# Gated cross-attention and mixture-of-experts block, one core: the value product cut into three key chunks in three consecutive slots, and the next batch's preparation laid out anew over the slots

## The chip, the cores and the metric

The kernel runs on 1 core of one Trainium2 chip. The metric is the device time of one execution in microseconds (us), lower is better. The engines are TensorE (PE; its weight loads are shown apart, as PEld), VectorE (DVE), ScalarE (ACT), GpSimd (POOL) and SyncE (SP, which only issues DMAs here).

## The reference

Cut to what matters. B = 16 batches, S = 112 queries, S2 = 375 keys, D = 256 columns, 16 heads of 16 columns.

```python
q = split_heads(layernorm(x) @ wq + bq); k = split_heads(ctx @ wk + bk); v = split_heads(ctx @ wv + bv)
logits = einsum('bhqd,bhkd->bhqk', q, k) / 4 + (1 - mask) * -1e9
attn = softmax(logits) * group_prob            # group_prob is per batch, query and key
out = einsum('bhqk,bhkd->bhqd', attn, v)       # the value product
x = x + tanh(g_xattn) * (out @ wo + bo)
x = x + tanh(g_ffn) * ffn(layernorm(x))        # a shared FFN and the two best of 8 experts
```

## The kernel before

The kernel has a prologue (queries, weights and batch 0's keys and values), the attention over 16 batches, and then the output projection, routing and the expert FFN. Only the attention and the lines ahead of it are touched.

**Steps and slots.** The attention has one `step` for each batch t on every engine, two steps to a loop iteration, and 16 slots n in a step, one for each head. The order of work on an engine is written out by hand, so an engine that waits holds up everything behind it. In slot n of TensorE's step stand: the three transposes of head n's probabilities (`turn_probs`, L925; float32, 112 rows by 125 keys, one for each third of the keys) into bank `PT[n % 2]`; between them the scores of head n + 4 (`scores`, L912) into bank `SC[n % 2]`; and one slot of the preparation of the next batch, in three thirds (`prep_third`). The transposes of head n wait until the bank has been read for head n - 2.

**The other engines.** In slot n VectorE masks the scores of head n + 3 and takes their row maximum (`mask_scores`, L1227), and multiplies the turned probabilities of head n by the turned group probabilities into `probsT` (`weigh`, L1234). ScalarE takes the exponentials (L713). For the four heads of `POOL_HEADS` GpSimd multiplies by the group probabilities before the transposes instead (`times_group_prob`, L508), TensorE's transposes wait for that, and ScalarE only copies the turned result (`copy_probs`, L704) two heads later in its own order.

**The value product.** `values` (L943) takes four heads (a quad) at once: 3 key chunks by 4 heads = 12 float32 matmuls, each on its own 32 columns of the array (125 x 32 weights, 112 columns streamed); the trace shows two instructions for each, so 24. It stands in slots 1, 5, 9 and 13, after the slot's preparation; in slot 1 it is the last quad of the batch before. In slot 5 the row sums are turned behind it (`turn_sums`, L900).

**The preparation of a batch** runs through two PSUM banks, `PR[0]` and `PR[1]`, in seven pieces: the context turned (`turn_ctx`, L842, two pieces of 6 float16 transposes), the keys (`keys`, L854, two pieces of 6 matmuls over 375 columns), the values (`vals`, L878, with a bias matmul L876 ahead of each of the three chunks of 6 matmuls; chunks 0 and 1 are one piece in `PR[1]`, chunk 2 a piece in `PR[0]`) and the group probabilities turned (`turn_gp`, L863, 3 transposes). ScalarE takes every piece out of PSUM (`prep_piece`: L639, L644, L651, L654, L647), and for the keys VectorE takes the low part as well (`keys_low`, L1180). The slot of a piece is that of `prep_slot` less `PREP` = 4: keys in slots 15 (of the step before), 0, 1 and 2; nothing in 3, 4 and 14; values in 5 to 10; group probabilities in 11; context of the batch after the next in 12 and 13. The keys' high and low parts go through DRAM (`store_keys`, L299) and come back stacked (`stack_keys`, L308) before the batch's scores.

Of the kernel before, what the change touches and what calls it, by code (L numbers as in the profile page):

```python
# [35 lines left out]
PREP = 4  # L36
# [25 lines left out]
def flamingo_block(nc, x, ctx, gp, mask, g_xattn, g_ffn, wq, bq, wk, bk, wv, bv, wo, bo, nw, router,  # L62
# [9 lines left out]
    with ExitStack() as st:  # L72
# [116 lines left out]
        prep_mm, prep_act, prep_lo = sem("prep_mm"), sem("prep_act"), sem("prep_lo")  # L189
# [35 lines left out]
        POOL_HEADS = (2, 6, 8, 12)  # L225
# [9 lines left out]
        def turned_ctx(k):  # L235

            return ps[:, PR[k], 0:KC * P].bitcast(F16).rearrange("p (a c n) -> p a c n", a=2, c=KC)
# [7 lines left out]
        def _(sp):  # L245
# [46 lines left out]
            def store_keys(b, m):  # L292
                high, low = sp.compute_val(7 * b + 3 + m), sp.compute_val(2 * b + 1 + m)
# [69 lines left out]
            def step(t, p, more=True):  # L363
# [255 lines left out]
        def _(act):  # L619
# [16 lines left out]
            def prep_piece(b, k, p):  # L636
                act.wait_ge(prep_mm, 7 * b + k + 1)
                if k < 2:
                    act.activation(ctxT[:, :, k, 0:S2].rearrange("p a (c n) -> p a c n", c=KC), turned_ctx(k)[:, :, :, 0:KP],  # L639
                                   ACT.Copy).then_inc(prep_act, 1)  # L640
                elif k < 4:
                    if not (isinstance(b, int) and b == 0):
                        act.wait_ge(k_out[k - 2], 48 * b)
                    act.activation(kT[:, HI, k - 2], bank(PR[k - 2], P, S2), ACT.Identity,  # L644
                                   bias=bcol[:, k:k + 1]).then_inc(prep_act, 1)
                elif k == 6:
                    act.activation(gpT[:, p], bank(PR[1], KP, KC * S).rearrange("p (c q) -> p c q", c=KC), ACT.Copy).then_inc(prep_act, 1)  # L647
                elif k == 4:
                    if isinstance(b, int) and b == 0:
                        act.wait_ge(pad_zero, 2)  # L650
                    act.activation(head_columns(p, 0, 2), bank(PR[1], KP, 2 * D).rearrange("p (c h d) -> p c h d", c=2, h=H),  # L651
                                   ACT.Copy).then_inc(prep_act, 1)
                else:
                    act.activation(head_columns(p, 2, 3), bank(PR[0], KP, D).rearrange("p (c h d) -> p c h d", c=1, h=H),  # L654
                                   ACT.Copy).then_inc(prep_act, 1)
# [37 lines left out]
            prep_piece(0, 6, 0)  # L693
# [13 lines left out]
            pieces = {0: 1, 3: 2, 5: 3, 11: 4, 13: 5, 14: 6}  # L707

            def step(t, p, first=False, t_next=True, t_after=True):
                act.wait_ge(rr_made, t + 1)  # L710
                for n in range(H):
# [12 lines left out]
            prep_piece(1, 0, 1)  # L724
            step(0, 0, first=True)
            with act.Fori(0, B // 2 - 2) as i:
                step(2 * i + 1, 1)
                step(2 * i + 2, 0)
            step(B - 3, 1)
            step(B - 2, 0, t_after=False)  # L730
            step(B - 1, 1, t_next=False, t_after=False)
# [70 lines left out]
        def _(pe):  # L802
# [28 lines left out]
            def turn_ctx(b, k, third):  # L831
                if third == 0:
                    if k == 0:
# [3 lines left out]
                        else:  # L837
                            pe.wait_ge(prep_act, 7 * b - 1)
                    elif not (isinstance(b, int) and b == 0):
                        pe.wait_ge(prep_act, 7 * b)  # L840
                for a in range(2):
                    mm = pe.transpose(turned_ctx(k)[:, a, third, 0:KP], ctx_pair[:, a, third, k * P:(k + 1) * P], ident16[0:KP, 0:KP])  # L842
# [3 lines left out]
            def keys(b, m, part, third):  # L846

                if third == 0:
                    if m == 0:
                        pe.wait_ge(prep_act, 7 * b + 1 + part)  # L850
# [3 lines left out]
                mm = pe.matmul(bank(PR[m], P, S2), wpair[:, 1, w, part, m * P:(m + 1) * P], ctxT[:, a, part, 0:S2],  # L854
# [4 lines left out]
            def turn_gp(b, p, n, third):  # L859
                if third == 0:  # L860
                    pe.wait_ge(in_gp[p], 16 * n)
                    pe.wait_ge(prep_act, 7 * b + 5)
                mm = pe.transpose(ps[0:KP, PR[1], third * S:(third + 1) * S], gp_in[:, p, third * KP:(third + 1) * KP], ident[0:S, 0:S])  # L863
# [3 lines left out]
            def vals(b, c, part, third):  # L867

                if c == 0 and part == 0 and third == 0:
                    pe.wait_ge(prep_lo, 2 * b + 2)  # L870
                    if isinstance(b, int) and b == 0:
                        pe.wait_ge(w_lo, 5)
                        pe.wait_ge(ctx_pad, 1)
                to = ps[:, PR[0] if c == 2 else PR[1], c % 2 * D:c % 2 * D + D]
# [54 lines left out]
            def values(t, g, p):  # L929

                if g == 0:
                    pe.wait_ge(o_read, t + 1)
                    pe.wait_ge(prep_act, 7 * t + 7)
                four = range(g * QUAD, (g + 1) * QUAD)
                pe.wait_ge(pt_read, NDVE * t + by_dve(four[-1]) + PT_FREE)
                pe.wait_ge(pt_copied, NPOOL * t + by_pool(four[-1]))
                for c in range(KC):
                    for k in four:

                        h = ORDER[k]  # L940
                        half, row = h // (H // ND), h % (H // ND) // 2 * PAD
                        first = h * PAD + (DH if h % 2 == 0 else 0)
                        mm = pe.matmul(ps[row:row + PAD, OB[p], half * S:(half + 1) * S], values_pad[p][:, c, first:first + PAD],  # L943
                                       probsT[:, k % AT, c], start=(h % 2 == 0 and c == 0), stop=(h % 2 == 1 and c == KC - 1))
                mm.then_inc(av_made, 1)
# [4 lines left out]
            for n in range(2):  # L950
                prep_whole(0, n, 0, 1)
            queries(0)
            for n in range(2, 7):
                prep_whole(0, n, 0, 1)
            turn_x(Q_TILES[1])
            for n in range(7, H - 1):
# [5 lines left out]
            prep_whole(0, H - 1, 0, 1)  # L962
# [9 lines left out]
            for n in range(2):  # L972
# [4 lines left out]
            def step(t, p, loads, loaded, loaded_next, first=False, t_next=True, t_after=True):  # L977

                def prep_third(n, third):
                    if n + PREP < H and t_next:  # L980
                        prep_slot(t + 1, n + PREP, 1 - p, loads, third)
                    if n + PREP >= H and t_after:
                        prep_slot(t + 2, n + PREP - H, p, None, third)
# [33 lines left out]
            values(B - 1, H // QUAD - 1, 1)  # L1017
# [103 lines left out]
        def _(dve):  # L1121
# [56 lines left out]
            def keys_low(b, m):  # L1178
                dve.wait_ge(prep_act, 7 * b + 3 + m)
# [291 lines left out]
```

## Time and profile before

| | before |
|---|---|
| median of 3 runs | 702.06 us (701.38 to 702.97) |
| the profiled execution's own time | 701.34 us |
| its span, first to last instruction | 699.5 us |
| mean granted TensorE clock | 0.952 |
| attention, first to last transpose of probabilities | 48.5 to 343.2 us |
| one step in the steady part | 18.8 us |

The times are those of the whole launch; the span is some 1.8 us less than the execution's own time. A row of a timeline gives the start in us from the span's start, the duration, the engine, the line, the operation, what it writes and reads, its shape, and (if there was any) the idle time of the engine before it with what ended it. Matmuls are pipelined: a duration of 0.26 us is a latency, and what a matmul costs TensorE is the distance from its start to the next one's.

### The profile page before, as it was taken

Reading aid. Unit: us, or ns where it says so; the run is one execution under the profiler, and the core shown is the slowest. Engines: PE = TensorE matmul, PEld = TensorE weight load, DVE = VectorE, ACT = ScalarE, POOL = GpSimd, SP = SyncE. Lnnn points to the kernel's source line nnn. Section 1 sums busy time; section 2 is a strip of 40 time slices with the busy share of each in tenths; the row PEclk is TensorE's granted clock in tenths of the full one; section 3 lists DMA queues with packets and bytes.
Section 4 is the critical chain, followed back from the end, with each engine's and each line's share of the span. In section 5 each row is a group of like instructions: output and inputs, shape, how many; then the busy total and the mean of one; then the engine's idle time right before and its main releaser. Section 6 shows DMA issues by size and latency. Waiting matters only on the chain. (4 is left out here: it accounts for less than half of the span.)

```text
span 699.5 us, 19174 instructions
## 1 busy us (share of the span) xinstructions
PE 598.9 (86%) x6150; PEld 499.4 (71%) x6150; DVE 482.4 (69%) x1298; ACT 392.8 (56%) x994; POOL 281.7 (40%) x327
## 2 busy tenths in 40 slices
PE   2689999999999999999757999898999999799960
PEld 2457777777777778777536887787788788587850
DVE  6858777877777877778695766547555556556537
ACT  4368888888888888887716423144352444424320
POOL 7303444443443334446530178605345525355120
PEclk9799999999999999999975999999999999999995
DMA  8536557775555555632040042203434332341218
GB/s 219 153 81 144 151 138 188 184 197 135 132 130 137 138 141 138 155 87 68 1 181 1 9 152 84 98 23 116 141 110 147 107 120 91 120 138 46 61 49 311
DMA packets 86601, 84.29 MB, mean 121 GB/s; under 512 B 17879, under 2 KB 80341, under 8 KB 86430
## 3 DMA queue, kind: packets, MB, share of 16 engines
q1 hardware_dynamic: 78686, 70.83, 36.8%
q0 software_dynamic: 2976, 8.16, 3.2%
q10 hardware_dynamic: 4896, 4.76, 2.5%
q8 instruction: 23, 0.38, 0.2%
q14 instruction: 20, 0.16, 0.1%
HBM read 55.43 MB, written 28.30 MB: 120 GB/s over the span
## 5 line engine op out<-in xcount | busy, mean ns | idle before, releaser
L925 PE MATMUL ps<-ident,probs 112*125 112x112 f32 x768 | 192.6, 277 | 2.5 <-POOL probs L508 1.4
L713 ACT ACTIVATE probs<-probs,negmax 112x375 f32<-112x375 f32 x256 | 154.9, 608 | 26.0 <-DVE negmax L1227 25.8
L1079 PE MATMUL ps<-w,arena 128*128 128x256 f16 x1152 | 139.0, 277 | 20.8 <-DVE arena L1370 20.6
L763 ACT ACTIVATE arena<-ps,b 128x256 f32<-128x256 f32 x192 | 78.5, 473 | 138.8 <-PE ps L1068 138.8
L925 PEld LDWEIGHTS ps<-ident,probs 112*125 112x125 f32 x768 | 138.9, 188 | 23.6 <-issue 7.4
L1227 DVE CUSTOM_DVE_ANT_0 probs<-ps,neg 112x375 f32<-112x375 f32 x256 | 137.3, 538 | 11.8 <-issue 9.5
L1079 PEld LDWEIGHTS ps<-w,arena 128*128 128x128 f16 x1152 | 109.9, 99 | 45.6 <-DVE arena L1370 32.2
L508 POOL TENSOR_TENSOR probs<-probs,gp_in 112x375 f32<-112x375 f32 x64 | 58.6, 915 | 181.2 <-ACT probs L713 181.1
L1234 DVE TENSOR_TENSOR arena<-ps,gpT 125x336 f32<-125x336 f32 x192 | 97.0, 506 | 46.3 <-PE ps L925 45.7
L1068 PE MATMUL ps<-probs,w 128*128 128x256 f16 x816 | 91.9, 273 | 0.0
L1068 PEld LDWEIGHTS ps<-probs,w 128*128 128x128 f16 x816 | 79.9, 98 | 9.2
L912 PE MATMUL ps<-kst,arena 112*128 112x375 f16 x256 | 82.7, 324 | 2.3 <-DVEq L1214 1.3
L1370 DVE TENSOR_TENSOR arena<-arena 128x512 f16<-128x512 f32 x96 | 73.9, 770 | 3.3
L611 POOL DMA_INDIRECT y_back<-y_sb,dest x34 | 36.5, 1073 | 72.9 <-DVE y_sb L1434 66.6
L1368 DVE CAST arena<-arena 128x512 f16<-128x512 f32 x96 | 46.0, 479 | 25.0 <-ACT arena L763 24.8
L878 PE MATMUL ps<-wpair,ctxT 128*128 128x256 f16 x288 | 62.5, 281 | 0.0
L592 POOL DMA_INDIRECT x_sent<-qT,slots x28 | 32.8, 1172 | 52.5 <-issue 52.5
L943 PE MATMUL ps<-arena,w 125*32 125x112 f32 x1536 | 50.1, 263 | 0.7 <-DVE arena L1234 0.7
L713 ACT ACTIVATION_READ_ACCUMULATOR probs<-probs,negmax 112x1 f32 x256 | 50.0, 195 | 0.0
L854 PE MATMUL ps<-ctxT,wpair 128*128 128x375 f16 x192 | 49.4, 330 | 0.0
L581 POOL CAST w<-w2s 128x512 f16<-128x512 f32 x32 | 20.8, 649 | 67.8 <-DVE arena L1370 61.4
L943 PEld LDWEIGHTS ps<-arena,w 125*32 125x32 f32 x1536 | 34.6, 109 | 13.7 <-issue 11.2
(173 smaller groups left out, 829.8 us busy)
## 6 DMA issues: line engine op xcount, KB each, us to landing
k_scratch<-kT SPq DMA_DIRECT2D x96, 93.8 KB
kst<-k_scratch SPq DMA_DIRECT2D x64, 140.6 KB, 3.5
w1s<-in_L_ffn_ew_dram SPq DMA_DIRECT2D x8, 1024.0 KB, 4.9
w2s<-in_L_ffn_ew_dram SPq DMA_DIRECT2D x8, 1024.0 KB, 5.6
x_sent<-y_sb SPq DMA_DIRECT2D x12, 516.0 KB, 5.1
ctx_in<-in_ctx_dram SPq DMA_DIRECT2D x16, 375.0 KB
probs<-x_sent ACTq DMA_DIRECT2D x18, 258.0 KB, 2.6
arena<-y_back SPq DMA_DIRECT2D x7, 512.0 KB, 7.1
```

The source lines that it names most:

```text
L508: pool.tensor_tensor(probs[:, n % PROBS], probs[:, n % PROBS], gp_in[:, p], ALU.mult).then_inc(gp_times, 1)
L713: act.activation(probs[:, n % PROBS], probs[:, n % PROBS], ACT.Exp, bias=negmax[:, p, n:n + 1], scale=-1.0, accum_out=rowsum[:, p, ORDER[n ...
L763: act.activation(hid32[:, f], ps[:, f // 2 % 4, f % 2 * TILE:(f % 2 + 1) * TILE], ACT.Relu, bias=b1[:, f, e:e + 1]).then_inc(h_relu, 1)
L878: mm = pe.matmul(to, ctxT[:, a, part, c * KP:c * KP + P], wpair[:, 2, w, part], start=False, stop=(part == 1 and third == 2))
L912: pe.matmul(bank(SC[n % 2], P, S2), qb[0:PAIR, p, h // 2, h % 2], kst[0:PAIR, p, h // 2], start=True, stop=True).then_inc(sc_made, 1)
L925: mm = pe.transpose(ps[0:KP, PT[n % 2], c * S:(c + 1) * S], probs[:, n % PROBS, c * KP:(c + 1) * KP], ident[0:S, 0:S])
L943: mm = pe.matmul(ps[row:row + PAD, OB[p], half * S:(half + 1) * S], values_pad[p][:, c, first:first + PAD], probsT[:, k % AT, c], start=(h ...
L1068: mm = pe.matmul(ps[:, f // 2 % 4, f % 2 * TILE:(f % 2 + 1) * TILE], w1[:, p, w, k, f * P:(f + 1) * P], rows(a, k), start=(j == 0), stop=( ...
L1079: mm = pe.matmul(ps[:, 4 + a, 0:D], hid[:, u, f, a * P:(a + 1) * P], w2[:, p, w, f], start=(f == 0 and j == 0), stop=(f == NF - 1 and j == 2))
L1227: dve.tensor_tensor_reduce(probs[:, n % PROBS], bank(SC[n % 2], S, S2), neg[:, p], -1.0, BIG, ALU.add, ALU.min, negmax[:, p, n:n + 1]).the ...
L1234: dve.tensor_tensor(probsT[:, n % AT], bank(PT[n % 2], KP, KC * S).rearrange("p (c q) -> p c q", c=KC), gpT[:, p], ALU.mult).then_inc(pt_r ...
L1370: dve.tensor_tensor(hid[:, LO, two], hid32[:, two], hid[:, HI, two], ALU.subtract).then_inc(h_split, 1)
```

## The change

The value product is cut: `values` takes one key chunk c (4 matmuls, one for each head of the quad), and the three chunks stand in slots 1, 2 and 3, in 5, 6 and 7, and so on. The preparation is laid out anew: keys in slots 0 to 3, values in 5 to 10 with chunk 2 first, the group probabilities in 11, the context of the batch after the next in 13 and 14, and nothing in 4, 12 and 15. Its seven pieces now take the two banks strictly in turn, over the border between batches too (`prep_bank`). The group probabilities are copied out of PSUM by VectorE in its slot 11 (`take_group_probs`), no longer by ScalarE. ScalarE's pieces, VectorE's low keys and division, and `POOL_HEADS` (1, 5, 9, 13) move to other slots. SyncE stores a piece of the keys in two parts (high ones first) and stacks the first half before it stores the second. The prologue has the same pieces in the new order.

```diff
-        POOL_HEADS = (2, 6, 8, 12)
+        POOL_HEADS = (1, 5, 9, 13)
+        def prep_bank(p, piece):
+            return PR[(p + piece) % 2]
...
 def store_keys(b, m):
-                sp.wait_ge(prep_lo, low)
                 for n, c in enumerate(K_PARTS):
+                    if c == LO:
+                        sp.wait_ge(in_x[0], 16)
+                        sp.wait_ge(prep_lo, low)
                     sp.dma_start(heads[:, n * DH:(n + 1) * DH], kT[:, c, m]).then_inc(k_out[m], 16)
...
-                for m in range(ND):
-                    store_keys(t + 1, m)
+                store_keys(t + 1, 0)
                 if more:
                     next_mask(t + 1, 1 - p)
-                for m in range(ND):
-                    stack_keys(t + 1, 1 - p, m)
+                stack_keys(t + 1, 1 - p, 0)
+                store_keys(t + 1, 1)
+                stack_keys(t + 1, 1 - p, 1)
...
-            pieces = {0: 1, 3: 2, 5: 3, 11: 4, 13: 5, 14: 6}
+            pieces = {0: 0, 1: 1, 3: 2, 5: 3, 8: 4, 12: 5}
...
-                    if t_after and n == H - 1:
-                        prep_piece(t + 2, 0, p)
-                    if n == 8 and not first:
+                    if n == 9 and not first:
                         take_sums(t - 1, 1 - p)
...
 def turn_ctx(b, k, p, third):
                         else:
-                            pe.wait_ge(prep_act, 7 * b - 1)
+                            pe.wait_ge(prep_act, 6 * b)
                     elif not (isinstance(b, int) and b == 0):
-                        pe.wait_ge(prep_act, 7 * b)
+                        pe.wait_ge(gp_turned, b)
...
+            V_ORDER = (2, 0, 1)
+            def vals(b, c, part, p, third):
+                if part == 0 and third == 0:
+                    if c == 2:
+                        pe.wait_ge(prep_lo, 2 * b + 1)
+                    if c == 0:
+                        pe.wait_ge(prep_lo, 2 * b + 2)
...
+            CTX_SLOTS, V_SLOT, GP_SLOT = (13, 14), 5, 11
             def prep_slot(b, n, p, loads, third):
-                if n < 2:
-                    turn_ctx(b, n, third)
-                elif 3 <= n < 7:
-                    keys(b, (n - 3) // 2, (n - 3) % 2, third)
-                elif 9 <= n < 15:
-                    vals(b, (n - 9) // 2, (n - 9) % 2, third)
-                elif n == 15:
+                if n in CTX_SLOTS:
+                    turn_ctx(b, CTX_SLOTS.index(n), p, third)
+                elif n < 2 * ND:
+                    keys(b, n // 2, n % 2, p, third)
+                elif V_SLOT <= n < GP_SLOT:
+                    vals(b, V_ORDER[(n - V_SLOT) // 2], (n - V_SLOT) % 2, p, third)
+                elif n == GP_SLOT:
                     turn_gp(b, p, loads, third)
...
-            def values(t, g, p):
-                if g == 0:
-                    pe.wait_ge(o_read, t + 1)
-                    pe.wait_ge(prep_act, 7 * t + 7)
+            def values(t, g, p, c):
                 four = range(g * QUAD, (g + 1) * QUAD)
-                pe.wait_ge(pt_read, NDVE * t + by_dve(four[-1]) + PT_FREE)
-                pe.wait_ge(pt_copied, NPOOL * t + by_pool(four[-1]))
-                for c in range(KC):
-                    for k in four:
-                        ...
-                mm.then_inc(av_made, 1)
+                if c == 0:
+                    if g == 0:
+                        pe.wait_ge(o_read, t + 1)
+                        pe.wait_ge(prep_act, 6 * t + 6)
+                    pe.wait_ge(pt_read, NDVE * t + by_dve(four[-1]) + PT_FREE)
+                    pe.wait_ge(pt_copied, NPOOL * t + by_pool(four[-1]))
+                for k in four:
+                    ...
+                if c == KC - 1:
+                    mm.then_inc(av_made, 1)
...
-                    if first and n == 0:
-                        for m in range(2, PREP):
-                            prep_whole(t + 1, m, 1 - p, loads)
...
-                    if n % QUAD == 1:
+                    if n % QUAD >= 1:
                         if n > QUAD:
-                            values(t, n // QUAD - 1, p)
+                            values(t, n // QUAD - 1, p, n % QUAD - 1)
                         elif not first:
-                            values(t - 1, H // QUAD - 1, 1 - p)
+                            values(t - 1, H // QUAD - 1, 1 - p, n % QUAD - 1)
...
-            values(B - 1, H // QUAD - 1, 1)
+            for c in range(KC):
+                values(B - 1, H // QUAD - 1, 1, c)
...
+            def take_group_probs(b, p):
+                dve.wait_ge(prep_mm, 7 * b + 7)
+                dve.tensor_copy(gpT[:, p], bank(prep_bank(p, 6), KP, KC * S).rearrange("p (c q) -> p c q", c=KC)).then_inc(gp_turned, 1)
...
-                    if prep and n in (1, 3):
-                        keys_low(t + 1, n // 3)
+                    if prep and n in (2, 5):
+                        keys_low(t + 1, n // 5, 1 - p)
+                    if prep and n == 11:
+                        take_group_probs(t + 1, 1 - p)
-                    if n == 8 and not first:
+                    if n == 9 and not first:
                         divide(t - 1, 1 - p)
```

## Rows read from the trace of the kernel before

**Rows 1.** The page's part 1: busy time of each engine.

```profile
PE 598.9 (86%) x6150; PEld 499.4 (71%) x6150; DVE 482.4 (69%) x1298; ACT 392.8 (56%) x994; POOL 281.7 (40%) x327
```

**Rows 2.** Windows, one for each step: busy us (x instructions) by engine, clock, DMA.

```profile
68.13:86.95 18.82, 17.65 (x212) 14.79 (x211) 14.79 (x49) 15.34 (x45) 7.79 (x10) 1.00 0.56 152
...
274.89:293.65 18.76, 17.60 (x213) 14.75 (x211) 14.79 (x49) 15.34 (x45) 7.78 (x10) 1.00 0.64 158
293.65:312.08 18.43, 17.34 (x212) 14.76 (x211) 14.70 (x49) 15.39 (x45) 7.80 (x10) 1.00 0.35 84
312.08:329.30 17.22, 16.43 (x197) 13.54 (x196) 14.62 (x49) 13.95 (x43) 10.36 (x12) 1.00 0.28 69
329.30:343.00 13.70, 12.09 (x156) 9.40 (x156) 11.87 (x41) 10.74 (x33) 8.58 (x10) 1.00 0.01 2
```

**Rows 3.** Waits from 100 to 300 us: us in total, times, longest.

```profile
PEld ps L842 <- ACT gpT L647: 8.4, 11, 0.8
PEld ps L876 <- DVE kT L1180: 8.1, 11, 0.8
```

**Rows 4.** TensorE's timeline, slot 1 of one step and the start of slot 2.

```profile
219.41 0.26 PE L925 MATMUL ps<-ident,probs 112*125 112x112 f32 x1
219.51 0.32 PE L854 MATMUL ps<-ctxT,wpair 128*128 128x375 f16 x1
219.68 0.26 PE L925 MATMUL ps<-ident,probs 112*125 112x112 f32 x1
219.77 0.32 PE L912 MATMUL ps<-kst,arena 112*128 112x375 f16 x1
219.93 0.26 PE L925 MATMUL ps<-ident,probs 112*125 112x112 f32 x1
220.03 0.48 PE L854 MATMUL ps<-ctxT,wpair 128*128 128x375 f16 x2
220.44 0.78 PE L943 MATMUL ps<-arena,w 125*32 125x112 f32 x24
221.15 0.36 PE L925 MATMUL ps<-ident,probs 112*125 112x112 f32 x1
221.35 0.32 PE L854 MATMUL ps<-ctxT,wpair 128*128 128x375 f16 x1
```

**Rows 5.** TensorE's timeline of the step before: slots 5 to 8, parts.

```profile
207.33 0.41 PE L900 MATMUL ps<-ident,rrow 112*128 112x112 f32 x2
207.58 0.27 PE L925 MATMUL ps<-ident,probs 112*125 112x112 f32 x1
...
208.37 0.26 PE L925 MATMUL ps<-ident,probs 112*125 112x112 f32 x1
...
209.27 0.26 PE L925 MATMUL ps<-ident,probs 112*125 112x112 f32 x1
...
210.05 0.26 PE L925 MATMUL ps<-ident,probs 112*125 112x112 f32 x1
```

**Rows 6.** TensorE's timeline of the same step: slots 10, 12 and 13, parts.

```profile
212.41 0.38 PE L878 MATMUL ps<-wpair,ctxT 128*128 128x256 f16 x2
...
213.56 0.36 PE L925 MATMUL ps<-ident,probs 112*125 112x112 f32 x1
...
214.29 0.39 PE L842 MATMUL ps<-ident,ctx_pair 125*128 125x125 f16 x4
214.52 0.31 PE L925 MATMUL ps<-ident,probs 112*125 112x112 f32 x1
```

**Rows 7.** ScalarE's timeline of the same step.

```profile
211.12 0.60 ACT L651 ACTIVATE w<-ps 125x512 f32<-125x512 f32 x1
211.59 0.62 ACT L713 ACTIVATE probs<-probs,negmax 112x375 f32<-112x375 f32 x1
...
212.83 0.38 ACT L654 ACTIVATE w<-ps 125x256 f32<-125x256 f32 x1
```

**Rows 8.** GpSimd's timeline of the same step: head 12.

```profile
212.45 0.99 POOL L508 TENSOR_TENSOR probs<-probs,gp_in 112x375 f32<-112x375 f32 x1 [2.12 <-ACT probs L713]
```

More of the change, by code:

```diff
@@ L704, in copy_probs, with step @@
                 act.activation(probsT[:, n % AT], bank(PT[n % 2], KP, KC * S).rearrange("p (c q) -> p c q", c=KC), ACT.Copy).then_inc(pt_copied, 1)
-            pieces = {0: 1, 3: 2, 5: 3, 11: 4, 13: 5, 14: 6}
-            def step(t, p, first=False, t_next=True, t_after=True):
+            pieces = {0: 0, 1: 1, 3: 2, 5: 3, 8: 4, 12: 5}
+            def step(t, p, first=False, t_next=True):
                 act.wait_ge(rr_made, t + 1)
@@ L853, in keys @@
                 w, a = PASSES[third]
-                mm = pe.matmul(bank(PR[m], P, S2), wpair[:, 1, w, part, m * P:(m + 1) * P], ctxT[:, a, part, 0:S2],
+                mm = pe.matmul(bank(prep_bank(p, 2 + m), P, S2), wpair[:, 1, w, part, m * P:(m + 1) * P], ctxT[:, a, part, 0:S2],
                                start=(part == 0 and third == 0), stop=(part == 1 and third == 2))
@@ L861, in turn_gp @@
                     pe.wait_ge(in_gp[p], 16 * n)
-                    pe.wait_ge(prep_act, 7 * b + 5)
-                mm = pe.transpose(ps[0:KP, PR[1], third * S:(third + 1) * S], gp_in[:, p, third * KP:(third + 1) * KP], ident[0:S, 0:S])
+                    pe.wait_ge(prep_act, 6 * b + 5)
+                mm = pe.transpose(ps[0:KP, prep_bank(p, 6), third * S:(third + 1) * S], gp_in[:, p, third * KP:(third + 1) * KP], ident[0:S, 0:S])
                 if third == KC - 1:
                     mm.then_inc(prep_mm, 1)
[L867 to L871, printed above, removed]
+            V_ORDER = (2, 0, 1)
[5 more added lines that the diff above has]
+                        pe.wait_ge(prep_lo, 2 * b + 2)
+                    if c == 2 and isinstance(b, int) and b == 0:
                         pe.wait_ge(w_lo, 5)
                         pe.wait_ge(ctx_pad, 1)
-                to = ps[:, PR[0] if c == 2 else PR[1], c % 2 * D:c % 2 * D + D]
+                to = ps[:, prep_bank(p, 4 if c == 2 else 5), c % 2 * D:c % 2 * D + D]
                 if part == 0 and third == 0:
@@ L927, in turn_probs @@
                     mm.then_inc(pt_made, 1)
-            def values(t, g, p):
-                if g == 0:
-                    pe.wait_ge(o_read, t + 1)
-                    pe.wait_ge(prep_act, 7 * t + 7)
+            def values(t, g, p, c):
                 four = range(g * QUAD, (g + 1) * QUAD)
-                pe.wait_ge(pt_read, NDVE * t + by_dve(four[-1]) + PT_FREE)
-                pe.wait_ge(pt_copied, NPOOL * t + by_pool(four[-1]))
-                for c in range(KC):
-                    for k in four:
[L940 to L944, printed above, removed]
-                mm.then_inc(av_made, 1)
+                if c == 0:
[5 more added lines that the diff above has]
+                for k in four:
+                    h = ORDER[k]
+                    half, row = h // (H // ND), h % (H // ND) // 2 * PAD
+                    first = h * PAD + (DH if h % 2 == 0 else 0)
+                    mm = pe.matmul(ps[row:row + PAD, OB[p], half * S:(half + 1) * S], values_pad[p][:, c, first:first + PAD],
+                                   probsT[:, k % AT, c], start=(h % 2 == 0 and c == 0), stop=(h % 2 == 1 and c == KC - 1))
+                if c == KC - 1:
+                    mm.then_inc(av_made, 1)
             pe.sem_inc(pt_made, PROBS_FREE)
@@ L949, in _ @@
             turn_x(Q_TILES[0])
-            for n in range(2):
+            for n in CTX_SLOTS:
                 prep_whole(0, n, 0, 1)
             queries(0)
-            for n in range(2, 7):
+            for n in range(2 * ND):
                 prep_whole(0, n, 0, 1)
             turn_x(Q_TILES[1])
-            for n in range(7, H - 1):
+            for n in range(V_SLOT, GP_SLOT):
                 prep_whole(0, n, 0, 1)
@@ L971, in _ @@
             mm.then_inc(small_T, 1)
-            for n in range(2):
+            for n in CTX_SLOTS:
                 prep_whole(1, n, 1, 1)
@@ L979, in prep_third @@
                 def prep_third(n, third):
[L980 to L983, printed above, removed]
+                    if n < CTX_SLOTS[0]:
+                        if t_next:
+                            prep_slot(t + 1, n, 1 - p, loads, third)
+                    elif t_after:
+                        prep_slot(t + 2, n, p, None, third)
                 for n in range(H):
                     turn_probs(t, n, 0)
-                    if first and n == 0:
-                        for m in range(2, PREP):
-                            prep_whole(t + 1, m, 1 - p, loads)
                     prep_third(n, 0)
@@ L1195, in _ @@
             for m in range(ND):
[L1196 removed]
+                keys_low(0, m, 0)
             weights_low(W_ORDER[2])
@@ L1208, in _ @@
                 queries_low(c)
+            take_group_probs(0, 0)
             dve.wait_ge(small_out, 4)
@@ L1230, in weigh @@
             def weigh(t, n, p):
+                if n == 0:
+                    dve.wait_ge(gp_turned, t + 1)
                 dve.wait_ge(pt_made, 16 * t + n + 1 + PROBS_FREE)
```

44 lines of the change are left out of this document (18 added, 26 removed).

## The prediction

> **What bounds it now.** I read the page's busy table first: TensorE is busy 86% of the span, VectorE 69%, ScalarE 56% [rows 1]. The change touches 48 to 343 us only, so I cut that stretch into its steps with the windows view. The twelve steps from 68.13 to 293.65 us take 225.5 us, 18.79 each; in one, TensorE is busy 17.6, ScalarE 15.3, VectorE 14.8, GpSimd 7.8 [rows 2]. Batch 13's step takes 18.43, batch 14's 17.22 (no later batch's context), the last 13.70 (no preparation, no scores for a next batch). A busy PE is not a PE at its peak, so I then looked at the waits: between 100 and 300 us TensorE's weight loads wait 11 times 0.76 us for ScalarE's copy of the turned group probabilities before the second context piece (slot 13), and 11 times 0.74 us for the second low keys before the values (slot 5) [rows 3]. To see the rest I priced TensorE's instructions by distance of starts in its timeline.
>
> **Prices.** A transpose of probabilities costs 0.09 to 0.10, a key matmul 0.16 to 0.17, a score matmul 0.16 [rows 4], so an empty slot is 3 x 0.10 + 0.16 = 0.46 and a key slot 0.46 + 3 x 0.157 = 0.93. A value slot is 0.78 (209.27 to 210.05), with its bias 0.90 [rows 5]; four context transposes cost 0.23 [rows 6], so a context slot is 0.46 + 6 x 0.055 = 0.79. The three group-probability transposes have the shape of the others, 0.31. `turn_sums` adds 0.25, less 0.09 since the transposes behind it then need no wait for their weights: 0.16 [rows 5]. The quad of values: the last key matmul starts at 220.03 + 0.16 and has streamed at 220.35; the first transpose after the quad starts at 221.15 and the next instruction 0.20 later, where 0.10 is usual [rows 4]. So a quad costs 221.35 - 220.35 - 0.10 = 0.90.
>
> Sum of a step without the quads: 16 empty slots 7.38, 12 key matmuls 1.88, 18 value matmuls 1.93 and 3 biases 0.33, group probabilities 0.31, context 0.66, sums 0.16: 12.66. Four quads 3.62: **16.28**. The step takes 18.79, so TensorE waits **2.5** in it: 1.5 are the two named waits (with the weight load that is then not hidden nearer 1.85), the rest are slots 3, 4, 11 and 12, short ones in which VectorE's mask and product or GpSimd's head 12 come last. VectorE and ScalarE stand idle for 4.0 and 3.5 us of it [rows 2], so TensorE is what the step runs by.
>
> **What the change removes.** Nearly all of these 2.5. The second context piece now waits for a copy that VectorE made two slots earlier. The values begin with chunk 2 in slot 5, which needs only the first low keys (VectorE's slot 2); the second are needed in slot 7 and made in 5. Empty slots no longer stand two in a row, and beside each stand slots lengthened by a chunk, so VectorE (0.9 a slot) keeps up.
>
> **What it adds on TensorE: eight more entries into the 32-column products.** A quad is 24 instructions whose starts span 0.78 - 0.26 = 0.52 us [rows 4], 0.022 apart, where one stream of 112 columns takes 0.09 to 0.10; so four run side by side, in six rounds. Six rounds are 6 x 0.096 = 0.58 of the 0.90. The other 0.33 lie at the borders: 0.09 from the last key matmul's end to 220.44, and behind the last round 0.1 of standstill and 0.1 of weights loaded in the open. A chunk keeps two rounds and the whole border: 0.90 - 4 x 0.096 = **0.52**. Twelve chunks are 6.24 where four quads were 3.62: **+2.6** a step. Bounds: nothing at the added borders gives 0.30 a chunk, the dearest reading of rounds (0.09) 0.55. I take 0.52, since in [rows 4] the border is the same kind of change of shape that each chunk makes, and I see nothing in those rows that ties a border's length to the number of rounds between. The Trainium skill (TensorEngine Tiling (Array Packing), Key Properties) says that changing the tiling mode drains TensorE, while changing only the tile does not. By that rule each of the 24 borders of a step is paid, as the trace's 8 are now, and the sum is the one above.
>
> So TensorE's own work is 12.66 + 6.24 = **18.90**, already 0.1 more than the whole step takes today.
>
> **What is late next.** I followed the chains by the new slots. ScalarE takes the last values piece (now the two-chunk one) behind exponential 12, and exponential 13 stands behind it; head 13 is now GpSimd's. From the start of slot 10's last value matmul: the piece starts 0.31 later (212.41 and 0.11 for the second of the pair, to 212.83 [rows 6, 7]), the next exponential 0.47 after it (211.12 to 211.59 [rows 7]), and from that exponential's start to the transpose that waits for GpSimd 1.97 (211.59, GpSimd at 212.45 for 0.99, TensorE at 213.56 [rows 6, 7, 8]). Together 2.75. TensorE gets from there to slot 13 in 0.11 + 0.52 + (0.77 + 0.52) + 0.46 = 2.38. So slot 13 waits 0.35, and 0.1 for open weights: **0.45**. Behind this transpose are queued the context pieces, the scores and all of slot 14; ScalarE's copy of head 13 moves with it. From slot 13 head 1 needs, by estimate, 0.9 until the transposes of head 13 are out, three instructions of ScalarE (copy, exponential 0, context piece) at its mean of 15.3 / 28 = 0.55 (28 instructions without the 16 reads of sums) [rows 2], and the 1.97: 4.5; TensorE reaches slot 1 after 2 x 1.31 + 0.98 + 0.93 = 4.5. So that is just met. For head 9 the same sum leaves 0.25 spare, for head 5 0.65. VectorE gets one 336-element copy, about 0.45 like a product of that shape, in 18.9 us in which it works 14.8; it stands while slot 12 and 13 run, and the masks behind it have a slot in hand. ScalarE loses the same. SyncE's queue: the keys are finished a slot later, but stacked half by half, and the scores that need them start in slot 12, some 8 us on; the low part's wait no longer holds up the high part. No cost. If that cover were gone, a stack's landing (3 to 4 us) would show in slot 12.
>
> **Sum.** A steady step: 18.90 + 0.45 = 19.35 against 18.79, +0.56; twelve of them **+6.7**. Batch 13: 19.35 - 18.43 = **+0.9**. Batch 14 has no context transposes (0.66): 18.69 - 17.22 = **+1.5**. The last step: TensorE's work is 16 x 0.46 - 4 x 0.16 + 6.24 + 0.16 = 13.1, under today's 13.70, whose waits are for GpSimd and VectorE (GpSimd's heads 6 and 8 stood close and now stand four apart): **0**. The first step and the prologue do the same work in another order, a pair of key pieces less at its start and a wait for the first context copies instead: **0**, half a microsecond either way. What follows the attention is not touched. In all **+9.1**. The profiled execution took 701.34, 0.72 under the median of the runs; 702.06 + 9.1 = **711**.
>
> **Rivals.**
> 1. *No new wait at slot 13* (ScalarE runs ahead and the chain is shorter than its rows): 18.90 a step: 12 x 0.11 + 0.5 + 1.0 = +2.8, **705**. For it: ScalarE has 3.5 us idle a step. Against: the chain begins with a piece that can't be earlier.
> 2. *More waits*: head 1's chain has no slack, and if each late head makes the next late, or VectorE's copy holds up the masks, another 0.5 a step, 14 steps: +7, **718**.
> 3. *The borders cost nothing more, the other side*: if a chunk between other matmuls enters and leaves in the shadow of its neighbours, three chunks cost a quad, 0.90. Then TensorE's work stays 16.28, with the new wait 16.73, and 12 x 2.06 + 1.7 + 1.1 = 27.5 are gained: **675**. It decides below a chunk of (18.79 - 12.66 - 0.45) / 12 = 0.47, with no wait at all below 0.51. Against it stand the 0.09 ahead of the quad and the 0.20 behind it in [rows 4].
> 4. *No difference*: chunk at 0.49 with half the wait; the gain and the price meet: **702**.
>
> **Chances.** Forecast (two borders paid per chunk, one new wait) 0.52, rival 1 0.16, rival 2 0.17, rival 3 and everything between it and the break-even 0.10, rival 4 0.05. The measurement tells 0.2% (1.4 us) from no change. Slower by more: 0.52 + 0.16 + 0.17 = 0.85; within: 0.05; faster: 0.10. The range goes from rival 1 with a chunk of 0.51 (704) to rival 2 (719); the unlikely fast side is left out. The forecast's own range is 707 to 715.
>
> **What would show it.** In the profile after: a steady step of 19.3 to 19.4; L943 in groups of 8 with a standstill before each and 0.20 after the first transpose behind each; TensorE's waits for the group-probability copy and the low keys gone; in slot 13 a wait of 0.3 to 0.5 for GpSimd's product; TensorE busy a larger share although the kernel is slower. The prediction is wrong if the distance from the last matmul before a chunk to the second one behind it is less than 0.7, with 0.78 expected behind a key matmul (the borders are cheaper), or if the steps show waits of over 0.5 that I did not list.

## The result and the profile after

| | before | after |
|---|---|---|
| median | 702.51 us (701.38 to 703.13, 4 runs) | 720.2 us (718.22 to 721.49, 4 runs) |
| ratio, 95% interval | | 1.0248 (1.0222 to 1.0273) |
| profiled execution, span | 701.34, 699.5 us | 719.99, 718.2 us |

The change makes the kernel 2.5% slower, 18 us. The forecast was 711 with a range of 704 to 719: the direction was right, the size was off by a factor of two, and the time lies just outside the range.

The windows view of the kernel after, one line for each step. The columns are those of [rows 2].

```profile
68.39:87.91 19.52, 19.33 (x215) 14.44 (x212) 15.50 (x50) 15.08 (x44) 8.07 (x11) 1.00 0.51 135
...
107.34:130.39 23.05, 20.96 (x214) 15.42 (x210) 15.43 (x50) 16.18 (x46) 8.98 (x11) 0.93 0.59 159
130.39:149.76 19.37, 19.33 (x214) 14.44 (x210) 15.26 (x50) 14.40 (x43) 6.81 (x10) 1.00 0.62 172
149.76:170.34 20.58, 19.41 (x214) 14.37 (x210) 15.47 (x50) 15.31 (x44) 8.29 (x11) 1.00 0.60 167
170.34:189.71 19.37, 19.32 (x214) 14.43 (x211) 15.26 (x50) 15.02 (x44) 7.48 (x11) 1.00 0.56 149
189.71:209.32 19.61, 19.43 (x214) 14.39 (x210) 15.47 (x50) 15.32 (x44) 8.30 (x11) 1.00 0.58 153
...
306.66:326.12 19.46, 19.35 (x214) 14.38 (x210) 15.39 (x50) 15.30 (x44) 8.32 (x11) 1.00 0.41 95
326.12:344.67 18.55, 18.55 (x203) 13.58 (x199) 15.26 (x50) 14.11 (x43) 10.24 (x13) 1.00 0.25 64
344.67:358.60 13.93, 13.52 (x154) 9.36 (x150) 12.05 (x40) 11.08 (x33) 8.71 (x10) 1.00 0.01 2
```

Two things are to be seen. The steady steps alternate between 19.37 and 19.61, against 18.76 and 18.82 in [rows 2], and TensorE is busy for all but 0.05 to 0.2 us of them: it hardly waits. And two steps stand out, those of batch 3 (23.05) and of batch 5 (20.58). In the step of batch 5 TensorE is busy for 19.41 us, as in its neighbours, so something was late there. In that of batch 3 it stands still for 2.1 us and is busy for 20.96 besides, at a mean granted clock of 0.93: behind the standstill the clock falls to its lower level of 1.2 GHz (0.52 in the row below), and the step's work takes 1.5 us longer than in the other long steps (19.43).

```profile
125.80:129.20 3.40, 3.40 (x29) 2.54 (x31) 1.58 (x7) 2.32 (x7) 0.32 (x1) 0.52 0.57 113
```

TensorE's timeline around a chunk, to be laid beside [rows 4]:

```profile
210.97 0.48 PE L851 MATMUL ps<-ctxT,wpair 128*128 128x375 f16 x2
211.38 0.40 PE L947 MATMUL ps<-arena,w 125*32 125x112 f32 x8
211.71 0.36 PE L929 MATMUL ps<-ident,probs 112*125 112x112 f32 x1
211.91 0.32 PE L851 MATMUL ps<-ctxT,wpair 128*128 128x375 f16 x1
```

From the end of the key matmul (210.97 + 2 x 0.16 = 211.29) there are 0.09 us until the chunk starts, and 0.20 from the first transpose behind it to the next instruction. A chunk costs 211.91 - 211.29 - 0.10 = 0.52, and so do the others of the step (0.53 behind the group probabilities, and 0.47 ahead of the row sums, where a whole quad costs 0.04 less too). TensorE's waits in the steady part (170.34 to 306.66 us, seven steps; us in total, times, longest):

```profile
PEld ps L947 <- issue: 15.0, 63, 0.3
PEld ps L929 <- issue: 15.0, 80, 0.4
...
PEld ps L929 <- DVE arena L1245: 1.2, 7, 0.2
PE ps L929 <- POOL probs L513: 0.6, 3, 0.2
```

The waits for the group-probability copy and for the low keys [rows 3] are gone. The time at the borders of the chunks shows as "issue", idle time of the weight loads that no other engine ended: 30 us in seven steps, 4.3 a step, where the same two rows come to 7.7 in seven steps of the kernel before.

Where the 18.7 us of span went, by the starts and ends of the steps:

| stretch | before | after | difference |
|---|---|---|---|
| to the first transpose | 48.47 | 47.38 | -1.1 |
| step of batch 0 | 19.66 | 21.01 | +1.4 |
| steps of batches 3 and 5, over a steady one of 19.47 | | | +4.7 |
| twelve steps of batches 1 to 12, the rest | 225.5 | 233.6 | +8.1 |
| steps of batches 13 and 14 | 35.65 | 38.01 | +2.4 |
| the last step and what follows to the last value product | 15.39 | 15.32 | -0.1 |
| after the attention | 354.8 | 358.2 | +3.4 |

### The profile page after: what moved, and what is told of

Its sections match the earlier page's. It is cut to its first block and busy times, and to the rows that moved or that the text cites. A ratio compares the mean times of both kernels' runs of the same rounds, so it can differ in the third digit from the quotient of the medians.

```text
span 718.2 us, 19273 instructions
## 1 busy us (share of the span) xinstructions
PE 630.5 (88%) x6150; PEld 496.4 (69%) x6150; DVE 490.2 (68%) x1314; ACT 390.3 (54%) x978; POOL 286.1 (40%) x327
## 5 line engine op out<-in xcount | busy, mean ns | idle before, releaser
L929 PE MATMUL ps<-ident,probs 112*125 112x112 f32 x768 | 205.1, 292 | 1.7 <-POOL probs L513 1.1
L1083 PE MATMUL ps<-w,arena 128*128 128x256 f16 x1152 | 141.1, 280 | 23.7 <-DVE arena L1383 23.5
L1083 PEld LDWEIGHTS ps<-w,arena 128*128 128x128 f16 x1152 | 111.4, 100 | 49.1 <-DVE arena L1383 33.9
L1236 DVE CUSTOM_DVE_ANT_0 probs<-ps,neg 112x375 f32<-112x375 f32 x256 | 135.5, 538 | 2.4 <-issue 1.1
L947 PE MATMUL ps<-arena,w 125*32 125x112 f32 x1536 | 76.4, 272 | 0.3 <-DVE arena L1245 0.3
L616 POOL DMA_INDIRECT y_back<-y_sb,dest x34 | 38.0, 1118 | 74.4 <-DVE y_sb L1447 68.1
L947 PEld LDWEIGHTS ps<-arena,w 125*32 125x32 f32 x1536 | 30.3, 108 | 38.4 <-issue 33.0
L851 PE MATMUL ps<-ctxT,wpair 128*128 128x375 f16 x192 | 51.8, 333 | 0.0
```

The costliest lines, as they stand in the source:

```text
L929: mm = pe.transpose(ps[0:KP, PT[n % 2], c * S:(c + 1) * S], probs[:, n % PROBS, c * KP:(c + 1) * KP], ident[0:S, 0:S])
L1083: mm = pe.matmul(ps[:, 4 + a, 0:D], hid[:, u, f, a * P:(a + 1) * P], w2[:, p, w, f], start=(f == 0 and j == 0), stop=(f == NF - 1 and j == 2))
L1236: dve.tensor_tensor_reduce(probs[:, n % PROBS], bank(SC[n % 2], S, S2), neg[:, p], -1.0, BIG, ALU.add, ALU.min, negmax[:, p, n:n + 1]).the ...
```

## The experiments

**How they are compared.** The time behind the attention varies between executions of the same kernel (below), and the runs were made on several chips. So each row gives the ratio to the kernel before on the same chip, and from its own profile the mean of the steps of batches 6 to 12, four of its slots (from the first transpose of a head to that of the next, median over batches 6 to 11; slots 8 and 12 alternate between two lengths in some kernels), and the attention's length, from the first transpose to the start of the last value product.

| kernel | ratio (95%) | steady step | slots 5, 8, 12, 13 | attention |
|---|---|---|---|---|
| before | 1 | 18.79 | 2.94, 0.78, 0.98, 2.46 | 296.2 |
| before with chunks | 1.0325 (1.0271 to 1.0378) | 20.20 | 1.92, 0.88, 0.94, 2.07 | 316.5 |
| after | 1.0248 (1.0222 to 1.0273) | 19.47 | 1.58, 0.88, 0.84, 1.38 | 312.6 |
| after, SyncE's old order | 1.0147 (1.0091 to 1.0204) | 19.47 | 1.58, 0.88, 0.84, 1.38 | 308.1 |
| the same, values pieces later | 1.0095 (1.0062 to 1.0128) | 19.18 | 1.58, 0.88, 0.56, 1.35 | 303.9 |
| old order, two parts | 1.0117 (1.0098 to 1.0136) | 19.20 | 1.83, 0.94, 1.26, 1.57 | 304.8 |
| after, whole quads | 1.0339 (1.0268 to 1.0410) | 19.69 | 2.05, 1.47, 1.78, 1.76 | 317.9 |
| whole quads, old order | 1.0194 (1.0170 to 1.0219) | 19.74 | 2.05, 1.47, 1.78, 1.76 | 311.6 |
| the same, values pieces later | 0.9918 (0.9891 to 0.9945) | 18.26 | 2.05, 0.78, 0.64, 2.17 | 291.2 |
| whole quads, old order, old heads | 0.9796 (0.9767 to 0.9826) | 17.48 | 2.03, 0.78, 0.72, 2.09 | 285.7 |
| the same, group probabilities copied later | 0.9746 (0.9707 to 0.9785) | 17.17 | 2.03, 0.78, 0.72, 1.76 | 277.6 |

**SyncE's order of before in the changed kernel.**

```diff
-                store_keys(t + 1, 0)
+                for m in range(ND):
+                    store_keys(t + 1, m)
                 if more:
                     next_mask(t + 1, 1 - p)
-                stack_keys(t + 1, 1 - p, 0)
-                store_keys(t + 1, 1)
-                stack_keys(t + 1, 1 - p, 1)
+                for m in range(ND):
+                    stack_keys(t + 1, 1 - p, m)
```

> The changed kernel with SyncE's order of before: both halves of the keys stored, then the mask, then both halves stacked. Transfer theory (the first half's stack ahead of the second half's store blocks SyncE's queue in the early batches, which also have query stores and zero sends): the steady step stays 19.5 us, the steps that make batches 4 and 6 ready fall from 23.0 and 20.6 to 19.5, total 720 - 4.8 = 715. Rival (those two steps are late for another reason, such as the load on the DMA engines): they stay late, 720.

The windows of its steps of batches 3 and 5:

```profile
106.73:126.40 19.67, 19.48 (x214) 14.38 (x210) 15.43 (x50) 15.38 (x44) 8.36 (x11) 1.00 0.72 191
145.78:165.39 19.61, 19.42 (x215) 14.37 (x211) 15.47 (x50) 15.31 (x44) 8.30 (x11) 1.00 0.59 142
```

The steady steps are the same to 0.01 us, and the two late ones are gone: the attention is 4.6 us shorter. The times are of another chip, on which the kernel before took 709.26; the ratio to it, 1.0091 to 1.0204, lies under the changed kernel's 1.0222 to 1.0273. Of the 4.6 us, 1.5 are the lower clock behind the wait: in both of these steps the granted clock is 1.00. SyncE's own timeline in the changed kernel's step of batch 3, which begins at 107.34, shows the mechanism:

```profile
105.19 0.80 SPq L313 DMA_DIRECT2D kst<-k_scratch  x2
106.09 3.86 SPq L331 DMA_DIRECT2D q_scratch<-qT  x6
...
113.78 3.29 SPq L304 DMA_DIRECT2D k_scratch<-kT  x3
117.18 0.51 SPq L263 DMA_DIRECT2D mask_in<-in_mask_BxSxS_ik_dram  x1
121.38 0.81 SPq L313 DMA_DIRECT2D kst<-k_scratch  x2
122.28 1.97 SPq L304 DMA_DIRECT2D k_scratch<-kT  x3
126.43 0.81 SPq L313 DMA_DIRECT2D kst<-k_scratch  x2
```

SyncE now waits for a landing twice in each step, one after the other: the first half's store lands before its stack (117.18 to 121.38), and only then is the second half stored and waited for. The last stack goes out 19 us after the start of this step, and still after 14 in the steady ones, where it went out after about 11 before. The first steps also have six query stores, and those from batch 2 on the zeros for the routing. There the queue falls behind: the next query load goes out 1.2, 2.1 and 5.1 us into the steps of batches 1, 2 and 3 (-1.8, -2.6 and 0.1 before). In the last of them the stack of batch 4's first keys follows at 14.0, and the scores that need it start at 17.6, 2.4 late. The trace puts a wait in that step (107 to 131 us) down to it:

```profile
PE ps L916 <- DMA kst<-k_scratch: 2.1, 1, 2.1
```

**Whole quads in the changed kernel.** The three chunks stand in slots 1, 5, 9 and 13 again, back to back.

```diff
-                    if n % QUAD >= 1:
-                        values(..., n % QUAD - 1)
+                    if n % QUAD == 1:
+                        for c in range(KC):
+                            values(..., c)
```

> The changed kernel with the three key chunks of the value product back to back in one slot of four, everything else as changed. Border theory (each entry into the 32-column products costs TensorE about 0.33 us, eight more of them a step are 2.6): a step of 19.5 - 2.6 = 16.9 if nothing else binds, total 720 - 15 x 2.6 = 681, somewhat more where the keys' late stack then shows in slot 12. Rival (the layout itself, the new banks and VectorE's copy hold the step): a step above 18.5, total above 705.

The expectation failed: no gain, 19.69 a step, as the rival had it (above 18.5). The borders are paid less often, and the time is spent waiting instead, 3.4 us a step above TensorE's 16.3. Two steps are late for the keys' stack here too (22.4 and 23.8), with the granted clock at 0.92 and 0.86 in them.

**The chunks alone, in the kernel before.** `values` and its calls as changed, nothing else.

> The kernel before with the value product in three slots alone. Border theory: TensorE's work goes from 16.3 to 18.9 us a step and the two waits for the low keys and the group-probability copy stay, since what they wait for moves with the slots: a step of 20.3 to 21, total 702 + 15 x 1.9 = 730. Rival (waits and chunks cover each other): a step of 19.0, total 706. If a chunk's borders cost nothing: at most 702.

Every steady step is 20.20 us, +1.41, a little under the expected range, and the kernel takes 732.49 us where the one before takes 709.26 on the same chip. Of the 2.6 us of borders 1.2 fall into waits that were there. Two chunks less in slot 5 are 0.38, and it shrinks by 1.02, from 2.94 to 1.92: TensorE's weight loads wait for the low keys for 1.4 us in seven steps, not 5.3. Most of the rest goes in the short waits of slots 3, 4, 11 and 12. Slot 13 shrinks by 0.39, from 2.46 to 2.07, which is only its two chunks, and the wait for the copy of the group probabilities is as it was (5.4 us in seven steps). In ScalarE's order that copy stands behind the one for head 12, for which it waits for TensorE's own transposes in slot 12 (1.04 us, to 224.64 in one step), so it moves back with the chunks. So a border is a cost where TensorE is the bound. It is free where TensorE waits, unless the wait moves along with it.

**Whole quads and SyncE's old order.** Both edits from above.

> Whole quads and SyncE's order of before, the rest as changed. Border theory: TensorE's work 16.3 us a step and 0.2 to 0.5 of waits at GpSimd's heads, a step of 16.9, total 702 - 15 x 1.8 = 675. Rival (VectorE's 15.3 us of work a step with its waits becomes the bound, as two slots without a value product follow one another again): a step of 17.8, total 688.

Neither 17 nor 17.8 but 19.74, and no late step: the late stacks were not what held the whole quads. The profile shows what did. TensorE, ScalarE and GpSimd around slot 12 of a step:

```profile
220.56 0.38 PE L929 MATMUL ps<-ident,probs 112*125 112x112 f32 x2
...
222.27 0.36 PE L929 MATMUL ps<-ident,probs 112*125 112x112 f32 x1 [1.07 <-POOL probs L513]
```

```profile
219.97 0.60 ACT L657 ACTIVATE w<-ps 125x512 f32<-125x512 f32 x1 [0.79 <-PE ps L880]
220.46 0.60 ACT L715 ACTIVATE probs<-probs,negmax 112x375 f32<-112x375 f32 x1
```

```profile
221.29 0.85 POOL L513 TENSOR_TENSOR probs<-probs,gp_in 112x375 f32<-112x375 f32 x1 [2.72 <-ACT probs L715]
```

ScalarE waits for the values piece (to 219.97), takes it, then exponential 13 (220.46); GpSimd multiplies head 13 (221.29), and TensorE's transposes of that head start at 222.27. It is the chain that the prediction followed, 1.81 us from exponential to transpose, and with nothing between the piece and the transposes but slots 11 and 12, TensorE stands for 1.07 us. The same happens at heads 9 and 1.

**The chain undone in two ways.** In the first GpSimd's heads are again (2, 6, 8, 12), so that exponentials 8 and 12 stand ahead of the pieces; in the second the heads stay and ScalarE takes the two values pieces one exponential later.

```diff
-        POOL_HEADS = (1, 5, 9, 13)
+        POOL_HEADS = (2, 6, 8, 12)
```

```diff
-            pieces = {0: 0, 1: 1, 3: 2, 5: 3, 8: 4, 12: 5}
+            pieces = {0: 0, 1: 1, 3: 2, 5: 3, 9: 4, 13: 5}
```

> Whole quads and SyncE's order of before in the new layout, with GpSimd's heads (2, 6, 8, 12) instead of (1, 5, 9, 13). Chain theory (with whole quads the new layout waits in slots 0, 8 and 12 because the exponentials of heads 1, 9 and 13 stand behind a fresh piece on ScalarE and then go through GpSimd): heads 8 and 12 no longer stand behind a piece, the waits of 0.65 and 1.3 us go, heads 2 and 6 keep a small one: a step of 17.3 to 17.9 instead of 19.76, attention 275 to 285 us long instead of 311.5, total 22 to 35 us under the same kernel with the new heads. Rival (VectorE's rate holds the layout with whole quads): a step of 19 or more.

> Whole quads, SyncE's order of before, GpSimd's heads as changed, but ScalarE takes the two values pieces one exponential later (behind exponentials 9 and 13). Chain theory: slot 8 falls from 1.40 to 1.54 to about 0.8, slot 12 from 1.71 to 1.85 to about 0.6, the step from 19.76 to 17.9. Rival (those slots wait for VectorE or for the bank itself): they stay within 0.2.

Both bear the chain out. The old heads bring the step to 17.48. The later pieces bring slot 8 from 1.47 to 0.78 and slot 12 from 1.78 to 0.64, and give 0.4 of that back in slot 13; 18.26 a step, not the 17.9 expected. What slot 13 waits for is VectorE's mask, which frees the bank for the scores and stands behind the copy of the group probabilities (VectorE copies at 209.82 and masks at 210.24 for 0.54):

```profile
210.84 0.33 PE L916 MATMUL ps<-kst,arena 112*128 112x375 f16 x1 [0.26 <-DVE negmax L1237]
```

The kernel with the old heads also has two late steps, those of batches 3 and 4 (18.47 and 22.16), with waits of 1.4 and 3.7 us for the keys' stack, although SyncE has its old order. The kernel with the later pieces has one, of 18.92 against 18.40, and the one at 19.74 a step none. That a shorter step leaves the queue less time is the likely cause; it was not tested.

**The later pieces with three chunks.**

> The changed kernel (three chunks), SyncE's order of before, and the two values pieces one exponential later. Chain theory: of the step's 19.49 only slot 12's wait of 0.21 to 0.35 can go, 19.2; TensorE's own work with 24 borders, 18.9, is the floor. If the borders were not the floor, the step would fall as in the kernel with whole quads.

```profile
200.96:220.09 19.13, 19.13 (x214) 14.40 (x211) 15.24 (x50) 14.88 (x44) 7.45 (x11) 1.00 0.61 137
```

Slot 12's wait goes, and TensorE is now busy for 19.13 of 19.13 us. What gave 1.5 us with whole quads gives 0.3 with chunks: here the borders are the floor.

**Two parts instead of three.** Chunks 0 and 1 in one slot, chunk 2 in the next.

> The changed kernel with SyncE's order of before and the value product in two parts (chunks 0 and 1 in one slot, chunk 2 in the next), 16 borders a step instead of 24. Border theory alone: 4 x 0.33 = 1.3 us less than with three chunks, a step of 18.2. Chain theory: a part of that is lost to longer waits in slots 8 and 12 (two less chunks between the piece and head 13's transposes, one more in front of head 9's): 18.6 to 19.2.

19.20, 0.27 under three chunks. Of the 1.3 us of borders saved, slot 12 takes back 0.5 in waits, slots 0 and 8 together 0.4, and slots 1 and 9, where the first transpose behind such a wait has its weights loaded in the open, 0.1. It lies at the dear end of the chain theory's 18.6 to 19.2.

**The group probabilities copied later,** in the kernel with whole quads and old heads.

```diff
-                    if prep and n == 11:
+                    if prep and n == 12:
                         take_group_probs(t + 1, 1 - p)
```

> Whole quads, SyncE's order and GpSimd's heads of before, and VectorE's copy of the turned group probabilities in its slot 12 (GpSimd's head, without a product on VectorE) instead of 11. Theory: in the kernel with the copy in slot 11, TensorE's slots 12 and 13 wait 0.26 and 0.4 us since the mask behind the copy frees the score bank late; with the copy behind that mask the step falls from 17.45 to 17.1, attention by some 5 us, total 684. Rival (the wait in slot 13 is for the values piece or for the keys' stack): the step stays at 17.4, total 689.

17.17 a step. Slot 12 keeps its wait, slot 13 loses 0.33 (2.09 to 1.76): it is the wait for the mask again. This kernel is 2.5% faster than the one before (0.9746, 0.9707 to 0.9785), the best of all: the new layout without its chunks, heads and SyncE order. Its steps of batches 2, 3 and 5 are still late by 1.4 each, with a wait for the keys' stack in slot 12.

**Both kernels once more.**

> The kernel before, unchanged, for its profile on this chip. If the time after the attention is the same from run to run, it is 354.8 us here too; if it varies, the 3.4 us by which it was longer in the changed kernel's profile are no effect of the change.

> The changed kernel, unchanged, for a second profile. Steady steps of 19.37 and 19.61 again. If the two late steps (batches 4 and 6) come from the order of SyncE's queue, they come back within some tenths; if they were an accident of one execution, they do not.

The windows of the kernel before behind the attention, first in its first profile, then in this one:

```profile
344.69:699.50 354.81, 295.34 (x2717) 251.04 (x2708) 213.72 (x448) 129.19 (x253) 136.26 (x132) 0.92 0.31 104
```

```profile
344.28:712.20 367.92, 301.88 (x2717) 252.41 (x2707) 212.03 (x448) 128.63 (x253) 139.01 (x132) 0.90 0.31 100
```

Same code, 13 us apart, on two chips; in the 13 profiles of this study the stretch behind the attention takes 354.8 to 377.1, and on one chip, in four kernels that differ in the attention alone, 356.5 to 362.3. The attention of the kernel before repeats to 0.1 us (296.22 and 296.35). The changed kernel's second profile has the two late steps again, the first of them longer: TensorE waits for the stack for 3.6 us there, and the granted clock is 0.86.

```profile
106.26:131.41 25.15, 21.59 (x215) 15.96 (x211) 15.52 (x50) 16.27 (x46) 8.93 (x11) 0.86 0.59 155
150.78:171.18 20.40, 19.40 (x214) 14.38 (x210) 15.47 (x50) 15.30 (x44) 8.26 (x11) 1.00 0.61 167
```

## Why the prediction was right and wrong

**The borders (right).** +2.6 us a step of TensorE's work was the term that set the sign, and a chunk is 0.52 us as computed. By the Trainium skill's rule (TensorEngine Tiling (Array Packing), Key Properties: changing the tiling mode drains TensorE) all 24 borders are paid, and the trace agrees: each chunk has its borders, be it behind key, value, context or probability work, 0.47 to 0.53 in all.

**The waits removed (right).** The step went from 2.5 us of waits to 0.2 to 0.4.

**The steady step (size slightly off).** 19.35 was forecast, 19.47 measured. Two errors partly cancel. TensorE's own work is 19.13 to 19.23 (the steps with the later pieces, which hardly wait) and not 18.90. The largest share lies in the context slots, 1.35 and 1.36 with their chunk, where the forecast's prices give 1.21 and 1.31 (the last 0.10 of a chunk falls into the slot behind it). They were priced from four context transposes in a row; the transpose of probabilities behind a pair of them was left at 0.10 and costs 0.15. The wait at head 13 was there, through the chain that was followed, but smaller: slot 12 is 0.77 or 0.91 against 0.56 without it, so 0.21 and 0.35, where 0.35 was forecast and 0.1 for the open weights behind it. At head 1, whose chain was said to be "just met", every second step has 0.1 more. Over twelve steps +8.1 instead of +6.7.

**SyncE's queue (wrong).** "No cost" is the step that failed: +4.7 us. The prediction looked at when the keys' data was made and when the scores needed it, and counted 8 us between them. It did not count how long SyncE's in-order queue stands between, with one landing waited for behind another, nor what else passes through that queue in the first steps. The sign that it named for this case, a wait for a stack in slot 12, is what the trace shows, 2.1 us in one step and 1.2 in another. Nor did it count what such a wait brings with it: of the 4.7 us, 3.3 are the two waits, and the rest is the lower clock behind the longer one. The experiment with the old order shows that it is this order.

**The first step and what comes before it.** "0, half a microsecond either way": -1.1 and +1.4, together +0.3, and that is luck. The first step has nine chunks where it had three quads, which by the prediction's own prices is 9 x 0.52 - 3 x 0.90 = +2.0, and the term of 0 left this out. In it TensorE is now busy for all of 21.01 us, at a granted clock of 0.84, where it was busy for 18.50 of 19.66 at 0.92. The two kernels with SyncE's old order that differ in the chunks alone take 20.86 and 19.99 for it. What made the attention start 1.1 us earlier was not followed; two profiles of one kernel differ by 0.5 and by 1.2 there.

**Behind the attention.** The code there is the same, and the prediction had no term for its 3.4 us; without them the profiled execution would lie at 716.6. No run shows that the change causes them. From ScalarE's second conversion of expert weights (L758 before, L755 after) to the end the changed kernel's profile takes 234.4 us where the kernel before took 229.5; but the second profile of the kernel before has 234.5, and the second of the changed one 230.3. Against this stands that the changed kernel's whole stretch was the longer one on both chips (358.2 to 354.8, 377.1 to 367.9), and that its four runs lie within 3.3 us and those of the kernel before within 1.8. So what makes this stretch vary stays open, and whether the change has a share in it.

Without this stretch and the queue, the sum comes to 710.4 + 1.4 + 0.3 = 712 in the profile's terms, inside the forecast's own range. Rival 2 (more waits, 718) named the right size by a wrong mechanism: the heads' chain cost less than forecast and not more. Rival 3 (the borders cost nothing) is excluded.

**What the prediction did not ask.** Whether the chunks serve as cover. In the new layout they do: with whole quads the step is 19.7, no shorter, because the heads given to GpSimd stand behind fresh pieces. The chunks fill those waits at a price that comes to the same. With heads placed ahead of the pieces the layout with whole quads is worth 1.3 us a step (1.6 with the later copy), and the chunks are the loss. Three chunks with those heads were not run.

## What to carry to other kernels

A change of array shape on TensorE has a fixed price at each border; cut such work into pieces only where the engine would otherwise wait, compare the price with the waits slot by slot, and leave out a wait whose cause moves back with the pieces. Where three engines hand one item on (ScalarE, GpSimd, TensorE here), keep anything that has to wait off the first engine's queue ahead of that item; moving it is cheaper than covering the wait. For a queue that issues transfers, add up over a whole step how long it stands waiting for landings, and check the step with the most other transfers, not the steady one. A wait there can cost more than its length, since the clock may fall behind it.

## What the hardware showed that was not expected

A transpose of probabilities (float32) straight behind two context transposes (float16, 0.055 us each) costs 0.15 us from its start to the next one's, where 0.10 is usual, in the kernel before as in the changed one, with no border near:

```profile
213.77 0.28 PE L842 MATMUL ps<-ident,ctx_pair 125*128 125x125 f16 x2
213.89 0.31 PE L925 MATMUL ps<-ident,probs 112*125 112x112 f32 x1
214.04 0.32 PE L912 MATMUL ps<-kst,arena 112*128 112x375 f16 x1
```

A standstill of TensorE can be followed by a stretch at the lower clock. Behind the wait of 2.1 us in the changed kernel's step of batch 3 the clock was at 1.2 GHz for 3.4 us, and the step took 23.05 us where its like take 19.61; in the second profile, with a wait of 3.6 us, it took 25.15 at a mean clock of 0.86. Behind the wait of 1.2 us in the step of batch 5, and behind those of 1.5 and 1.6 in the fastest kernel, the granted clock stayed at 1.00, and the steps were longer by 1.0 and 1.4 us.

And an unchanged kernel's stretch behind the attention took 354.8 us in one execution and 367.9 in another. Ahead of its fourth conversion of expert weights ScalarE stood idle for 5.5 us in the first and 9.9 in the second; in the changed kernel's two profiles it is the other way about, 10.0 and 5.6. So a difference of a few us in one profile has to be placed by stretch before it is put down to a change.
